# Expert probabilities in groups of four batches: one softmax in place over the probabilities' tile

## The chip, the core and the metric

The kernel runs on one core of a Trainium2 chip. The metric is device time in microseconds (us) of one execution. Engines: PE is TensorE, DVE is VectorE, ACT is ScalarE, POOL is GpSimd, SP is SyncE, whose queue issues most of the DMA.

## The reference, cut to what matters

x and ctx are 32 batches of 512 tokens by 512 features. Two residual steps follow each other:

```python
x = x + tanh(g_xattn) * xattn(layernorm(x), ctx, ctx)    # 8 heads, gated scores with a decay per position
x = x + tanh(g_ffn)   * experts(layernorm(x))

# in experts(), on xf = all 16384 rows:
logits = xf @ Wr + br                 # 8 experts
Sm = softmax(logits, axis=-1)
G_t, idx_t = top_k(Sm.T, n_tok // 8)  # each expert takes the 2048 rows with the highest probability
out = silu(xf[idx] @ W_up + b_up) @ W_down + b_down
y[idx] += G * out
```

The experts can choose only when the probabilities of all rows are known.

## The kernel before, in words

The program has two stages, each a block in which every engine runs its own hand-written instruction list; an engine enters the second block when all have left the first.

**Attention stage.** A batch is 4 tiles of 128 tokens. A loop of 34 iterations (`for i in range(NB + 2)`, NB = 32) works on several batches at once: in iteration i batch i is loaded and gets its first row moments, b1 = i-1 is turned and gets its gates, b2 = i-2 gets its scores and products, b3 and b4 are normalised, the finished rows of b5 = i-5 are turned (`turn_rows`) and multiplied by the router weights (`logits`), and b6 = i-6 gets its softmax. After the loop a written-out tail finishes the last batches. The order of work on every engine is that of the code. PE's outputs go through four shared PSUM banks; `iteration_fills` lists who fills which bank and which engine ("act" or "dve") empties it, and `fill` makes PE wait for that engine before the bank is filled again.

The softmax of a batch: PE computes the logits with experts along partitions (`logits`), ACT adds the bias (`logit_rows`, tile lg), PE turns them one iteration later (`turn_logits`, L689) into a bank with tokens along partitions. DVE takes the maximum of each row and subtracts it (`shifted_logits`, L921 and L922, tile lt, 128x32), ACT takes the exponential (`exponentials`, L436, tile ex), DVE sums, inverts and multiplies (`probabilities`, L927 to L929) into sm_all, which holds the probabilities of all 16384 rows as 128 x 128 x 8. SP stores each batch's part of it into the last 8 columns of the row scratch in DRAM (`store_probabilities`, L264): 512 pieces of 32 bytes.

Other names that the prediction uses: L281 and L285 load ctx (kraw) and x (xs) on SP, the first once PE has finished the last `chunk_state` (L777) of i-2; L903 is `row_moments` (bn_stats); L1006 and L1007 are `turned_gates`, which read what PE's `turn_gates` (L722 to L724) wrote; L915 is `head_sums`, L1035 `chunk_states` (tile S), L738 `scores`, L1052 and L1055 are in `gate_runs`. Scores of pair 1 wait for S, because they share the banks that S is read from.

**Expert stage.** PE turns the score columns of sm_all, DVE and PE select each expert's 2048 rows by rounds of counting, POOL gathers the rows with their probabilities (it waits for all row stores and all probability stores) and adds the results to the output; weights are loaded on SP and split by ACT, POOL and DVE into two parts each.

Of the kernel before, what the change touches and what calls it, by code (L numbers as in the profile page):

```python
# [26 lines left out]
AX = mybir.AxisListType  # L27
# [23 lines left out]
CRING = 3  # L51

# [36 lines left out]
def attention(nc, io, NB, dram, sm_all, tg, consts, stored, plan):  # L89
# [4 lines left out]
    xf_v = dram["xf"].rearrange("(b j p) w -> b p j w", j=TILES, p=P)  # L94
    ident, identb, ones = consts["ident"], consts["identb"], consts["ones"]
    with ExitStack() as ctx:
# [6 lines left out]
        def sem(name):  # L103
# [34 lines left out]
        lt = sb("lt", [P, TILES, NEXP]); mx = sb("mx", [P, TILES]); sx = sb("sx", [P, TILES]); ex = sb("ex", [P, TILES, NEXP])  # L138
# [11 lines left out]
                 "ldg rp x2t xf2v dchain achain pchain prep1 prep2 prep3").split()  # L150
# [9 lines left out]
        def iteration_fills(i):  # L160
            b1, b2, b5, b6 = i - 1, i - 2, i - 5, i - 6

            plan = [("qw", b2, 0, "dve", 0), ("q", b1, 0, "act", 1), ("k", b1, 0, "act", 2), ("q", b1, 1, "act", 3), ("k", b1, 1, "act", 1),
                    ("st", b2, 0, "act", 0), ("st", b2, 1, "dve", 2), ("st", b2, 2, "dve", 3), ("xfT", b5, 0, "act", 1),
                    ("qw", b2, 1, "dve", 0), ("scores", b2, 1, None, None), ("xfT", b5, 1, "act", 1),
                    ("xfT", b5, 2, "act", 0), ("q", b1, 2, "act", 2), ("k", b1, 2, "act", 3), ("q", b1, 3, "act", 1),
                    ("lt", b6, 0, "dve", 0), ("xfT", b5, 3, "act", 2), ("k", b1, 3, "act", 3),
                    ("qw", b2, 2, "dve", 1), ("scores", b2, 2, None, None), ("shift", b1, 0, "dve", 1), ("qw", b2, 3, "dve", 1),
                    ("gates", b1, 0, "dve", 0), ("lg", b5, 0, "act", 1), ("turn", b1, 0, "dve", 1)]
            if i >= NB + 2:  # L170
                free = [n for n in range(4) if n != {NB + 2: 0, NB + 3: 3, NB + 4: 2}[i]]
                plan = [("lt", b6, 0, "dve", 0)] if i == NB + 2 else []
                plan += [("xfT", b5, c, "act", free[c % 3]) for c in range(CH)]
                plan += [("lg", b5, 0, "act", free[1]), ("lt", b5, 0, "dve", {NB + 2: 3, NB + 3: 2, NB + 4: 3}[i])]
            return [f for f in plan if live(f[1])]
# [36 lines left out]
        def wait_taken(eng, kind, b, k):  # L212

            eng.wait_ge(*freed[kind, b, k])

# [32 lines left out]
        with nc.Block() as block:  # L248
            @block.sync
            def _(sp):  # L250
# [10 lines left out]
                def store_probabilities(b):  # L261
                    if 0 <= b < NB:
                        sp.wait_ge(s["smx"], b + 1)
                        sp.dma_start(xf_v[b][:, :, E_DIM:XW], sm_all[:, b * TILES:(b + 1) * TILES, :]).then_inc(s_probs, 16)  # L264
# [158 lines left out]
            def _(act):  # L423
# [9 lines left out]
                def exponentials(b):  # L433

                    wait_taken(act, "lt", b, 0)
                    act.activation(ex[:, :, :], lt[:, :, :], ACT.Exp).then_inc(s["lex"], 1)  # L436
# [113 lines left out]
                for i in range(NB + 2):  # L550
# [27 lines left out]
                    if live(b1):  # L578
                        turned("q", b1, 2)
                        turned("k", b1, 2)  # L580
                        turned("q", b1, 3)
                    if live(b5):
                        turned_rows(b5, 3)
# [5 lines left out]
                    if live(b6):  # L589
                        exponentials(b6)  # L590
# [39 lines left out]
                exponentials(a - 2)  # L630
# [3 lines left out]
                second_norm(a, (0, 1, 2, 3))  # L634
                for c in range(CH):
                    turned_rows(a, c)
                rsqrt_guess(NB + 3)
                second_norm(b, (0,))
                exponentials(a - 1)
                logit_rows(a)  # L640
                exponentials(a)
# [3 lines left out]
                exponentials(b)  # L645
# [235 lines left out]
            def _(dve):  # L881
# [42 lines left out]
                def probabilities(b):  # L924

                    dve.wait_ge(s["lex"], b + 1)
                    step(dve.tensor_reduce(sx[:, :], ex[:, :, :], AX.X, ALU.add))  # L927
                    step(dve.reciprocal(sx[:, :], sx[:, :]))
                    dve.tensor_tensor(sm_all[:, b * TILES:(b + 1) * TILES, :], ex[:, :, :], spread(sx[:, :], 2, NEXP), ALU.mult).then_inc(s["smx"], 1)  # L929
# [156 lines left out]
                for i in range(NB + 2):  # L1086
# [25 lines left out]
                    if live(b6):  # L1112
                        shifted_logits(b6)
# [22 lines left out]
                    if live(b6):  # L1136
                        probabilities(b6)
# [18 lines left out]
                shifted_logits(a - 2)  # L1156
# [330 lines left out]
def experts(nc, io, dram, sm_all, slots, weights, tg, consts, stored, plan, NTOK, K):  # L1487
# [7 lines left out]
    with ExitStack() as ctx:  # L1495
# [60 lines left out]
        with nc.Block() as block:  # L1556
# [21 lines left out]
            def _(pool):  # L1578
# [14 lines left out]
                pool.wait_ge(stored["probs"], 16 * (NTOK // SEQ))  # L1593
# [241 lines left out]
```

## Time and profile before

| what | value |
|---|---|
| median of three runs | 3066.34 us (3066.11 to 3068.3) |
| span of the profiled execution, first to last instruction | 3068.9 us |
| attention stage in it, until PE's first instruction of the expert stage | 1013.4 us |
| loop iterations 5 to 31, from one L915 to the next | 28.89 to 33.33 us |
| PE, DVE, ACT, POOL busy over the span | 96%, 60%, 37%, 34% |

Rows of the profile give the start of an instruction, its duration, engine, line, operation, output<-input and, in brackets, how long the engine was idle before it and what ended that. Durations of a group are means in ns. A matmul's end is modelled, so a busy PE can hide short stalls.

### The profile page before, as it was taken

What the parts mean: (1) busy time and instruction counts of PE and PEld (TensorE: products, weight loads), DVE (VectorE), ACT (ScalarE), POOL (GpSimd) and SP (SyncE); (2) the same over time, 40 slices, a digit from 0 to 9 for tenths busy, and PEclk for the clock granted to TensorE, in tenths of its full rate; (3) what the DMA queues carried; (4) which work ended last, traced back from release to release, by engine and by line L of the source; (5) the groups of instructions that cost most, each with busy time, mean ns of one, the idle gap of its engine ahead of it and who ended that gap; (6) DMA issues with size and microseconds to landing.
All of it is one profiled execution on the core that took longest, in us unless ns stands there. A gap on an engine that the chain in (4) does not pass through costs nothing.

```text
span 3068.9 us, 60770 instructions
## 1 busy us (share of the span) xinstructions
PE 2960.4 (96%) x24708; PEld 2392.9 (78%) x24708; DVE 1830.2 (60%) x5124; ACT 1136.7 (37%) x2025; POOL 1057.8 (34%) x1029
## 2 busy tenths in 40 slices
PE   6999999999998599999999999999999999999998
PEld 5888888888886377877777787777777777777886
DVE  6999899999888644354454444544445445443332
ACT  5778787777776321121121121122112112112110
POOL 4777677777767311121111111121112111121111
PEclk9999999999999699999999999999999999999999
DMA  3243443434342521241142231232123214222121
GB/s 130 84 167 128 152 144 136 167 112 167 113 166 85 147 51 34 36 100 32 40 105 35 49 79 34 37 87 70 31 37 84 49 30 110 37 49 58 35 37 24
DMA packets 140062, 250.70 MB, mean 82 GB/s; under 512 B 31456, under 2 KB 31456, under 8 KB 139784
## 3 DMA queue, kind: packets, MB, share of 16 engines
q1 hardware_dynamic: 105784, 170.80, 16.6%
q0 software_dynamic: 28672, 67.65, 12.6%
q10 hardware_dynamic: 5328, 8.36, 0.9%
q8 instruction: 197, 3.23, 0.4%
q14 instruction: 81, 0.66, 0.1%
HBM read 137.23 MB, written 101.19 MB: 78 GB/s over the span
## 4 chain that ended last, share of the span: by engine, by line
PE 64%; DVE 1%; DMA 1%; issue 0%; ACT 0%; POOL 0%; ACTq 0%; DVEq 0%; POOLq 0%
PE DN L1713 32%; PE UP L1687 31%; PE TT L1660 1%; DMA w_raw<-in_L_ffn_W_down 1%; DVE c_hit L1380 0%; PE c_bank L1373 0%; PE c_bank L1357 0%; DVE c_hit L1401 0%; DVE c_within L1396 0%; DVE down_lo L1246 0%; POOL out_x L1606 0%; ACT z L1631 0%; DVE c_gained L1433 0%; DVE c_begun L1395 0%; DVE mid_lo L1745 0%
## 5 line engine op out<-in xcount | busy, mean ns | idle before, releaser
L1606 POOL DMA_INDIRECT out_x<-y,slots x128 | 201.9, 1578 | 1631.2 <-DVE y L1767 1631.2
L1713 PE MATMUL DN<-down_hi,mid_hi 128*128 128x512 f32 x1408 | 577.9, 410 | 0.0
L1631 ACT ACTIVATE z<-UP,bup 128x512 f32<-128x512 f32 (+1 forms) x352 | 240.7, 686 | 857.6 <-PE UP L1687 838.5
L1687 PE MATMUL UP<-xT_hi,up_lo 128*128 128x512 f32 (+1 forms) x1408 | 555.5, 395 | 0.0
L1687 PE MATMUL UP<-xT_hi,up_hi 128*128 128x512 f32 (+1 forms) x1408 | 554.0, 394 | 1.2 <-DVE xT_lo L1724 0.9
L1687 PE MATMUL UP<-xT_lo,up_hi 128*128 128x512 f32 (+1 forms) x1408 | 552.1, 392 | 0.0
L1713 PE MATMUL DN<-down_lo,mid_hi 128*128 128x512 f32 x1280 | 505.5, 395 | 0.0
L1713 PE MATMUL DN<-down_hi,mid_lo 128*128 128x512 f32 x1280 | 505.4, 395 | 0.0
L1743 DVE CAST mid_hi<-z 128x512 fp32r<-128x512 f32 (+1 forms) x352 | 151.2, 429 | 486.0 <-ACT z L1631 485.8
L1615 ACT ACTIVATE xT_hi<-TT 128x512 fp32r<-128x512 f32 x126 | 75.0, 596 | 690.9 <-PE TT L1660 670.9
L1687 PEld LDWEIGHTS UP<-xT_hi,up_hi 128*128 128x128 f32 (+1 forms) x1408 | 260.2, 185 | 68.5 <-ACT z L1631 4.2
L1687 PEld LDWEIGHTS UP<-xT_lo,up_hi 128*128 128x128 f32 (+1 forms) x1408 | 259.8, 185 | 67.3 <-issue 0.3
L1687 PEld LDWEIGHTS UP<-xT_hi,up_lo 128*128 128x128 f32 (+1 forms) x1408 | 260.0, 185 | 65.5 <-issue 0.5
L1713 PEld LDWEIGHTS DN<-down_hi,mid_hi 128*128 128x128 f32 x1408 | 265.6, 189 | 51.3
L1713 PEld LDWEIGHTS DN<-down_hi,mid_lo 128*128 128x128 f32 x1280 | 240.4, 188 | 57.9
L1765 DVE TENSOR_TENSOR y<-DN,bdn 128x512 f32<-128x512 f32 x128 | 88.6, 692 | 329.0 <-PE DN L1713 325.6
L1713 PEld LDWEIGHTS DN<-down_lo,mid_hi 128*128 128x128 f32 x1280 | 241.1, 188 | 45.5
L1745 DVE TENSOR_TENSOR mid_lo<-z,mid_hi 128x512 fp32r<-128x512 f32 (+1 forms) x352 | 244.0, 693 | 12.1
L233 POOL TENSOR_TENSOR nsb<-nsb,rr 128x512 f32<-128x512 f32 x125 | 126.9, 1046 | 231.1 <-DVE nn L960 231.1
L1017 DVE SCALAR_TENSOR_TENSOR C<-QK,C 128x512 f32<-128x512 f32 x256 | 164.8, 685 | 8.6 <-PE QK L738 6.5
L903 DVE BATCH_NORM_STATS2 st<-xs 128x6 f32<-128x512 f32 x248 | 152.9, 679 | 20.6 <-DMA xs<-in_x 20.5
L738 PE MATMUL QK<-qT,kT 64*128 64x128 f32 x2048 | 148.8, 285 | 14.2 <-DVE S L1035 13.0
(264 smaller groups left out, 4983.7 us busy)
## 6 DMA issues: line engine op xcount, KB each, us to landing
xs<-in_x SPq DMA_DIRECT2D x32, 1024.0 KB, 8.4
kraw<-in_ctx SPq DMA_DIRECT2D x32, 1024.0 KB, 5.6
out_x<-xs SPq DMA_DIRECT2D x32, 1024.0 KB, 12.8
rows_scratch<-xfb SPq DMA_DIRECT2D x32, 1024.0 KB, 11.4
w_raw<-in_L_ffn_W_down SPq DMA_DIRECT2D x40, 512.0 KB
w_raw<-in_L_ffn_W_up SPq DMA_DIRECT2D x16, 682.5 KB
mid_hi<-mid_hi ACTq DMA_DIRECT2D x32, 86.0 KB
mid_lo<-mid_hi ACTq DMA_DIRECT2D x32, 84.0 KB
```

What stands on the lines that cost most here:

```text
L233: ins = eng.tensor_tensor(n, n, spread(scale[:, j, :], 2, DH), ALU.mult)
L738: mm = pe.matmul(QK[:, par, jj], kT[r, b % 2, p, jj], qT[r, b % 2, p, jj], start=True, stop=True)
L903: dve.bn_stats(st[:, which, j, :], src[:, j, :]).then_inc(s["dchain"], 1)
L1017: dve.scalar_tensor_tensor(out=c, in0=QK[:, par, :], scalar=DH ** -0.5, in1=c, op0=ALU.mult, op1=ALU.mult)\
L1606: pool.indirect_dma_start(out_rows, bass.IndirectOffsetOnAxis(ap=slots[:, m:m + 1], axis=0), y[:, t, :], None, compute_op=ALU.add).then_in ...
L1615: act.activation(xT[0][:, c, :], turned(n, c)[:, :], ACT.Copy).then_inc(s["thi"], 1)
L1631: act.activation(z[0:r, k % 2, :], UP[k % 3][0:r, :], ACT.Silu, bias=bup[0:r, e // 2, f:f + 1]).then_inc(s["z"], 1)
L1687: mm = pe.matmul(UP[k % 3][0:r, :], weights.up[wa][:, c, f * P:f * P + r], xT[xa][:, c, :], start=first, stop=(c == CH - 1 and wa == 1))
L1713: mm = pe.matmul(DN[m % 2][:, :], lhs, rhs, start=first, stop=(f == FCH - 1 and lhs is parts[-1][0]))
L1743: dve.tensor_copy(mid[0][0:r, f, :], z[0:r, k % 2, :]).then_inc(s["hi"], 1)
L1745: dve.tensor_tensor(mid[1][0:r, f, :], z[0:r, k % 2, :], mid[0][0:r, f, :].bitcast(FP32), ALU.subtract)\
L1765: dve.tensor_tensor(y[:, t, :], DN[m % 2][:, :], bdn[:, e % 2, :], ALU.add).then_inc(s["yp"], 1)
```

## The change

The softmax works on groups of four batches (SOFT = 4). For every batch ACT now copies the turned logits from the bank straight into the batch's part of sm_all (`raw_logits`); the bank is thus emptied by ACT, not by DVE. In every fourth iteration DVE and ACT do maximum, subtraction, exponential, sum, reciprocal and product over 128x128 elements in place in sm_all, and SP stores the four batches with one DMA of 2048 pieces of 32 bytes. In the tail the last group (batches 28 to 31) is done after the last batch's logits. The tiles lt and ex go away, and the wait of POOL's gather counts 8 stores instead of 32.

```diff
+    xf_t = dram["xf"].rearrange("(t p) w -> p t w", p=P)
...
-                    ("lt", b6, 0, "dve", 0), ("xfT", b5, 3, "act", 2), ("k", b1, 3, "act", 3),
+                    ("lt", b6, 0, "act", 0), ("xfT", b5, 3, "act", 2), ("k", b1, 3, "act", 3),
...
+        def logits_of(g):
+
+            return sm_all[:, g * SOFT * TILES:(g + 1) * SOFT * TILES, :]
...
                 def store_probabilities(b):
-                    if 0 <= b < NB:
-                        sp.wait_ge(s["smx"], b + 1)
-                        sp.dma_start(xf_v[b][:, :, E_DIM:XW], sm_all[:, b * TILES:(b + 1) * TILES, :]).then_inc(s_probs, 16)
+                    if b >= 0 and b % SOFT == SOFT - 1:
+                        g = b // SOFT
+                        sp.wait_ge(s["smx"], g + 1)
+                        sp.dma_start(xf_t[:, g * SOFT * TILES:(g + 1) * SOFT * TILES, E_DIM:XW], logits_of(g)).then_inc(s_probs, 16)
...
-                def exponentials(b):
-
-                    wait_taken(act, "lt", b, 0)
-                    act.activation(ex[:, :, :], lt[:, :, :], ACT.Exp).then_inc(s["lex"], 1)
+                def raw_logits(b):
+
+                    t = filled(act, "lt", b, 0)
+                    act.activation(sm_all[:, b * TILES:(b + 1) * TILES, :], t[:, 0:P].rearrange("p (j n) -> p j n", n=QD)[:, :, 0:NEXP], ACT.Copy)\
+                       .then_inc(s["ta"], 1)
+
+                def exponentials(g):
+
+                    act.wait_ge(s["lsh"], g + 1)
+                    act.activation(logits_of(g), logits_of(g), ACT.Exp).then_inc(s["lex"], 1)
...
                         turned("q", b1, 3)
+                    if live(b6):
+                        raw_logits(b6)
                     if live(b5):
                         turned_rows(b5, 3)
...
-                    if live(b6):
-                        exponentials(b6)
+                    if live(b6) and b6 % SOFT == SOFT - 1:
+                        exponentials(b6 // SOFT)
...
-                def shifted_logits(b):
-
-                    t = filled(dve, "lt", b, 0)
-                    l3 = t[:, 0:P].rearrange("p (j n) -> p j n", n=QD)[:, :, 0:NEXP]
-                    step(dve.tensor_reduce(mx[:, :], l3, AX.X, ALU.max))
-                    dve.tensor_tensor(lt[:, :, :], l3, spread(mx[:, :], 2, NEXP), ALU.subtract).then_inc(s["td"], 1)
+                def shifted_logits(g):
+
+                    wait_taken(dve, "lt", g * SOFT + SOFT - 1, 0)
+                    step(dve.tensor_reduce(mx[:, :], logits_of(g), AX.X, ALU.max))
+                    dve.tensor_tensor(logits_of(g), logits_of(g), spread(mx[:, :], 2, NEXP), ALU.subtract).then_inc(s["lsh"], 1)
...
+                def probabilities(g):
+
+                    dve.wait_ge(s["lex"], g + 1)
+                    step(dve.tensor_reduce(sx[:, :], logits_of(g), AX.X, ALU.add))
                     step(dve.reciprocal(sx[:, :], sx[:, :]))
-                    dve.tensor_tensor(sm_all[:, b * TILES:(b + 1) * TILES, :], ex[:, :, :], spread(sx[:, :], 2, NEXP), ALU.mult).then_inc(s["smx"], 1)
+                    dve.tensor_tensor(logits_of(g), logits_of(g), spread(sx[:, :], 2, NEXP), ALU.mult).then_inc(s["smx"], 1)
...
-                    if live(b6):
-                        shifted_logits(b6)
+                    if live(b6) and b6 % SOFT == SOFT - 1:
+                        shifted_logits(b6 // SOFT)
...
-                    if live(b6):
-                        probabilities(b6)
+                    if live(b6) and b6 % SOFT == SOFT - 1:
+                        probabilities(b6 // SOFT)
...
-                probabilities(a - 2)
-                shifted_logits(a - 1)
                 reciprocal_roots(NB + 3)
                 last_norm(b)
-                probabilities(a - 1)
-                shifted_logits(a)
-                probabilities(a)
-                shifted_logits(b)
-                probabilities(b)
+                shifted_logits(b // SOFT)
+                probabilities(b // SOFT)
...
-                pool.wait_ge(stored["probs"], 16 * (NTOK // SEQ))
+                pool.wait_ge(stored["probs"], 16 * (NTOK // (SEQ * SOFT)))
```

## Rows read from the trace of the kernel before

**Rows 1.** The page, busy time of each engine over the span.

```profile
PE 2960.4 (96%) x24708; PEld 2392.9 (78%) x24708; DVE 1830.2 (60%) x5124; ACT 1136.7 (37%) x2025; POOL 1057.8 (34%) x1029
```

**Rows 2.** Windows of single iterations: length, busy by engine, clock, DMA share, GB/s.

```profile
123.91:152.80 28.89, 28.89 (x488) 24.54 (x487) 26.46 (x73) 23.50 (x46) 22.09 (x23) 1.00 0.42 148
449.78:478.94 29.16, 28.79 (x490) 24.55 (x489) 27.27 (x79) 23.62 (x47) 21.68 (x23) 1.00 0.43 147
629.45:659.95 30.50, 29.40 (x491) 24.74 (x489) 27.55 (x78) 23.66 (x48) 21.15 (x23) 1.00 0.41 140
597.72:629.45 31.73, 30.38 (x487) 25.54 (x486) 27.58 (x79) 23.10 (x46) 22.39 (x23) 0.95 0.40 135
```

**Rows 3.** Waits from 152.8 to 968: total us, times, longest.

```profile
DVE st L903 <- DMA xs<-in_x: 15.6, 17, 1.9
PE QK L738 <- DVE S L1035: 11.5, 24, 0.6
```

**Rows 4.** Timeline of DVE in the iteration 449.78 to 478.94.

```profile
460.33 0.19 DVE L921 TENSOR_REDUCE mx<-T 128x4 f32<-128x32 f32 x1
460.75 2.47 DVE L903 BATCH_NORM_STATS2 st<-xs 128x6 f32<-128x512 f32 x4
...
474.94 0.18 DVE L927 TENSOR_REDUCE sx<-ex 128x4 f32<-128x32 f32 x1
475.37 0.19 DVE L929 TENSOR_TENSOR sm_all<-ex,sx 128x32 f32<-128x32 f32 x1
475.48 0.33 DVE L1006 COPY gb<-T 64x8 f32<-64x8 f32 x2
```

**Rows 5.** Timeline of PE in the same iteration.

```profile
453.86 1.16 PE L738 MATMUL QK<-qT,kT 64*128 64x128 f32 x16 [0.37 <-DVE S L1035]
...
459.24 0.27 PE L689 MATMUL T<-ident,lg 128*128 128x128 f32 x1
459.35 0.60 PE L672 MATMUL QK<-ident,xfb 128*128 128x128 f32 x4
...
462.80 0.43 PE L698 MATMUL T<-qT,gW 128*32 128x128 f32 x8
...
474.87 0.29 PE L724 MATMUL T<-steps,ones 128*128 128x16 f32 x2
```

**Rows 6.** DMA issues, single iterations (from 272.46, 451.4, 597): last number us to landing.

```profile
xs<-in_x SPq DMA_DIRECT2D x1, 1024.0 KB, 8.3
...
xs<-in_x SPq DMA_DIRECT2D x1, 1024.0 KB, 8.0
...
xs<-in_x SPq DMA_DIRECT2D x1, 1024.0 KB, 9.7
```

**Rows 7.** Groups by line, 152.8 to 968: total busy us, mean ns, idle before.

```profile
L935 DVE TENSOR_REDUCE ssq<-sq 128x8 f32<-128x512 f32 x110 | 74.7, 680 | 1.0
L929 DVE TENSOR_TENSOR sm_all<-ex,sx 128x32 f32<-128x32 f32 x27 | 9.1, 337 | 0.9
L522 ACT ACTIVATE low<-low 128x128 f32<-128x128 f32 x27 | 8.4, 310 | 0.9
L1052 DVE TENSOR_TENSOR rise<-T,cs 128x128 f32<-128x128 f32 x27 | 7.9, 292 | 5.0 <-PE T L706 4.1
```

**Rows 8.** Timeline of ACT, same iteration as rows 4.

```profile
460.53 0.65 ACT L441 ACTIVATE kT<-QK 128x512 f32<-128x512 f32 x1
```

**Rows 9.** Timeline of DVE at the end of the attention stage.

```profile
1011.28 0.19 DVE L921 TENSOR_REDUCE mx<-QK 128x4 f32<-128x32 f32 x1 [3.95 <-PE QK L689]
...
1012.43 0.19 DVE L929 TENSOR_TENSOR sm_all<-ex,sx 128x32 f32<-128x32 f32 x1
```

**Rows 10.** Timeline of SP's queue in the iteration of rows 4.

```profile
454.62 2.22 SPq L264 DMA_DIRECT2D rows_scratch<-sm_all  x1
```

**Rows 11.** DMA queues from 1010 to 1014: packets, MB, share of 16 engines.

```profile
q1 hardware_dynamic: 551, 0.02, 6.8%
```

**Rows 12.** Timeline of POOL: the first gather of the expert stage.

```profile
1040.91 1.27 POOL L1585 DMA_INDIRECT xg<-rows_scratch,slots  x1 [6.04 <-DVE slots L1408]
```

More of the change, by code:

```diff
@@ L51 @@
 CRING = 3
+SOFT = 4
 class Line:
@@ L137, in attention @@
         N1, N2 = TILES * HEADS, TILES * HEADS + TILES
-        lt = sb("lt", [P, TILES, NEXP]); mx = sb("mx", [P, TILES]); sx = sb("sx", [P, TILES]); ex = sb("ex", [P, TILES, NEXP])
+        mx = sb("mx", [P, SOFT * TILES]); sx = sb("sx", [P, SOFT * TILES])
         gwr = C[0:16, 0:3, :].rearrange("g n e -> g (n e)")
@@ L149, in attention @@
                  "ee dd qk cc af an sq sr x2 x2v lex smx hs vc uv "
-                 "ldg rp x2t xf2v dchain achain pchain prep1 prep2 prep3").split()
+                 "ldg rp lsh x2t xf2v dchain achain pchain prep1 prep2 prep3").split()
         s = {n: sem("a_" + n) for n in names}
@@ L171, in iteration_fills @@
                 free = [n for n in range(4) if n != {NB + 2: 0, NB + 3: 3, NB + 4: 2}[i]]
-                plan = [("lt", b6, 0, "dve", 0)] if i == NB + 2 else []
+                plan = [("lt", b6, 0, "act", 0)] if i == NB + 2 else []
                 plan += [("xfT", b5, c, "act", free[c % 3]) for c in range(CH)]
-                plan += [("lg", b5, 0, "act", free[1]), ("lt", b5, 0, "dve", {NB + 2: 3, NB + 3: 2, NB + 4: 3}[i])]
+                plan += [("lg", b5, 0, "act", free[1]), ("lt", b5, 0, "act", {NB + 2: 3, NB + 3: 2, NB + 4: 3}[i])]
             return [f for f in plan if live(f[1])]
@@ L629, in _ @@
                 rsqrt_guess(NB + 2)
-                exponentials(a - 2)
+                raw_logits(a - 2)
                 for c in range(CH):
@@ L634, in _ @@
                 second_norm(a, (0, 1, 2, 3))
+                raw_logits(a - 1)
                 for c in range(CH):
@@ L638, in _ @@
                 second_norm(b, (0,))
-                exponentials(a - 1)
                 logit_rows(a)
-                exponentials(a)
+                raw_logits(a)
                 for c in range(CH):
@@ L644, in _ @@
                 logit_rows(b)
-                exponentials(b)
+                raw_logits(b)
+                exponentials(b // SOFT)
             @block.tensor
@@ L915, in head_sums @@
                     dve.tensor_reduce(hs[:, :], kraw[:, b % VBUF, :, :].rearrange("p j (h d) -> p (j h) d", d=DH), AX.X, ALU.add).then_inc(s["hs"], 1)
-                def shifted_logits(b):
-                    t = filled(dve, "lt", b, 0)
-                    l3 = t[:, 0:P].rearrange("p (j n) -> p j n", n=QD)[:, :, 0:NEXP]
-                    step(dve.tensor_reduce(mx[:, :], l3, AX.X, ALU.max))
-                    dve.tensor_tensor(lt[:, :, :], l3, spread(mx[:, :], 2, NEXP), ALU.subtract).then_inc(s["td"], 1)
-                def probabilities(b):
-                    dve.wait_ge(s["lex"], b + 1)
-                    step(dve.tensor_reduce(sx[:, :], ex[:, :, :], AX.X, ALU.add))
+                def shifted_logits(g):
[5 more added lines that the diff above has]
+                    step(dve.tensor_reduce(sx[:, :], logits_of(g), AX.X, ALU.add))
                     step(dve.reciprocal(sx[:, :], sx[:, :]))
-                    dve.tensor_tensor(sm_all[:, b * TILES:(b + 1) * TILES, :], ex[:, :, :], spread(sx[:, :], 2, NEXP), ALU.mult).then_inc(s["smx"], 1)
+                    dve.tensor_tensor(logits_of(g), logits_of(g), spread(sx[:, :], 2, NEXP), ALU.mult).then_inc(s["smx"], 1)
                 def square_sums(b, p):
@@ L1155, in _ @@
                 row_variances(NB + 2)
-                shifted_logits(a - 2)
                 weigh_early(b, 3)
```

## The prediction, made before the changed kernel was run

> **What bounds the kernel now.** I read the busy shares first [rows 1]: PE works 96% of the span, so at most the rest can be won by work on other engines. The change touches only the attention stage (1013.4 of 3068.9 us); the expert stage after it runs the same instructions. So I cut the loop into iterations, from one L915 to the next, and read PE, DVE and DMA in each [rows 2].
>
> The reader should see two kinds of iteration. In the short kind (449.78) PE is busy 28.79 of 29.16 us and DVE 27.27. DVE looks nearly as full, but PE's only idle time is 0.37 us, at L738, where the scores wait for DVE's S [rows 2, 5]. In the long kind (629.45, 30.50 us) DVE stands 1.4 us waiting for the load of xs, and PE then idles for DVE's results. Over the whole loop the load costs DVE 15.6 us in 17 waits, and S costs PE 11.5 us in 24 [rows 3].
>
> The best evidence is iteration 5 (123.91), which has everything but the softmax, since no batch has come that far: 28.89 us, PE busy 28.89 [rows 2]. With the turning of the logits, 0.11 us on PE (459.24 to 459.35 in [rows 5]), an iteration without DVE's softmax would take 29.00 us. The short kind takes 29.16.
>
> The long kind follows the landing of xs. That load is issued about 0.9 us behind the ctx load, which waits for PE's L777, and landed 7.9 to 9.9 us after its issue in 25 loads: 9 by 8.2 us, 4 at 8.3, 3 at 8.6 to 8.7, 9 at 9.1 or later (8.0, 8.3 and 9.7 in [rows 6]). Iterations with 8.0 took 29.16, with 8.3 some 29.3, with 9.4 some 30.4. This cycle runs from L777 through both loads, DVE's row moments (L903), the variances, `gate_runs` and PE's work back to L777. DVE's `shifted_logits` lies ahead of its wait for xs, and `probabilities` lies where PE has work in hand up to L777. Neither is on that cycle.
>
> **What is removed from DVE.** `shifted_logits`: from 460.33 to 460.75, 0.42 us. `probabilities`: from 474.94 to 475.48, 0.54 us, up to about 0.8 where the product is longer, its mean being 0.337 against 0.19 here [rows 4, 7]. Together 0.96 us. There are 28 softmax iterations in the loop, 6 to 33; the seven with i = 9, 13 ... 33 get a group, 21 get nothing.
>
> What 0.96 us is worth is read at two places. After `probabilities` DVE does L1006, which needs PE's L724; that ended at 474.87 + 0.29 = 475.16. So DVE can come forward from 475.48 to about 475.20 and then stands: 0.28 us, not 0.54. From there to S nothing else waits, so PE's 0.37 at L738 falls by 0.28; by the floor of iteration 5 it is 29.16 - 29.00 = 0.16. I take 0.2, bounds 0.16 and 0.28. The 0.42 us ahead of row moments turns into a longer wait for xs, or into DVE waiting for PE's L706 (4.1 us already [rows 7]). Value: nothing; it is covered by PE, and if PE were faster it would be worth up to 0.42.
>
> So over the 21: nine PE-bound ones (i = 6, 7, 8, 14, 15, 16, 24, 26, 32) at 0.2 make 1.8 us; three with landings of 8.3 (10, 27, 30) at 0.1, since their cycle binds at about 29.2, make 0.3; nine bound by the load, nothing. Sum -2.1, bounds -1.4 and -3.4.
>
> **What is added on DVE.** Widening from 128x32 to 128x128. The reduction costs 191 ns for 32 elements and 680 for 512, which is 1.02 ns an element, so +0.10 for 96 more; the subtraction and the product go from 0.19 to the 0.292 of L1052 [rows 4, 7]. Reciprocal 4 to 16 elements: nothing visible. `probabilities` thus grows by 0.2 and `shifted_logits` by 0.2 in seven iterations. The first comes out ahead of S, where PE waits already: +0.2 in the PE-bound ones (9, 17, 25, 33), 0.8 us. In 13, 21, 29 it lies off the load's cycle. The second is covered by DVE's slack at L706 and L768. Bounds: 0 and, with 0.4 in all seven, 2.8.
>
> **What is added on ACT.** 28 copies of 128x32 at about the 0.25 us of the exponential they replace, now between q's third copy and the row copies, and in seven iterations an exponential of 128x128 at 0.310 (L522 in [rows 7]). PE next needs kT's last copy for the gates: it ended at 461.18, PE came at 462.80 [rows 5, 8]. Slack 1.6 us against 0.25: nothing. Behind it on ACT are the squares and the third C exponential, used by DVE only near 465; the bank becomes free earlier than before. DVE's group start waits for the fourth copy, which ACT does at about 460.06 to 460.31, as DVE arrives: 0 to 0.1, inside the bounds above.
>
> **SP and the stores.** The store behind a full queue holds SP for 2.22 us [rows 10]; four times the pieces hold it some 9. Behind it is only the next iteration's ctx load, 24 us later. Pieces are cheap: 551 packets took 6.8% of 16 engines for 4 us, 7.9 ns each [rows 11], so 2048 take 1.0 us. They come behind xs in the queue and leave its landing alone. Nothing, bounds 0 and 0.
>
> **The tail.** The earlier softmaxes there fell into DVE's wait for ACT and PE; no gain. The last one is serial. Before: from 1011.28 to 1012.62, 1.34 us [rows 9]. After: copy 0.25, maximum 0.28, subtraction 0.29, exponential 0.31, sum 0.28, reciprocal 0.18, product 0.29, and six hand-overs of 0.03 to 0.04, in all 2.1. So +0.75, bounds +0.5 and +1.1. The last store sends 2048 pieces ahead of the first weights. Even at 9 us for its descriptors the gather at 1040.91 is not held by it; the weights' split on POOL has 6.04 us of idle time before that gather [rows 12].
>
> **Sum.** -2.1 + 0.8 + 0.75 = -0.55 us, bounds -2.9 and +2.5 before the loads and PE's clock move. Those do: the same loads cost 0 or 1.5 us in neighbouring iterations for no reason that the rows show. The profiled span of 3068.9 is 2.6 above the median (its upper run 3068.3), so I apply the difference to the median: 3066.34 - 0.55 = 3065.8 us. Own range 3061 to 3070.5.
>
> **Rivals.**
>
> *DVE sets the loop.* Its 93% busy speaks for it. Then the whole is worth 21 x 0.96 = -20.2, groups 7 x 0.4 = +2.8, tail +0.75: -16.6, 3049.7 us. Against it: PE has 0.37 us left. Chance 0.08. The Trainium skill (VectorE: DVE Perf Modes, the TRN2 errata) says small instructions reading SBUF each pay a fixed extra time, to be mended by larger tiles; the trace agrees in size (191 ns for 32 elements, 680 for 512), and by that rule alone the time would be this rival's.
>
> *The loads fall better.* DVE and SP are freer in 21 iterations; if half of the 15.6 us of waits went, -7.8 - 0.55: 3058. For it: landings of 8.0 and 9.8 alternate. Against: nothing that the change moves stands ahead of xs. Chance 0.12.
>
> *Slower: the clock falls at the groups.* The 31.73 us iteration had PE idle 1.35 us and then PE at 1.2 instead of 2.4 GHz for part of it (mean 0.95); 629.45 had 1.1 idle and kept its clock [rows 2]. A group adds 0.2 to the wait at S. If that tips PE in all seven at 31.73 - 30.50 = 1.2 us each, +8.4, and -0.55: 3074. It decides where the idle time passes between 1.1 and 1.35 us. Against: four groups meet iterations with 0.4 idle. Chance 0.11.
>
> *Slower: the last store holds the weights.* If its descriptors hold SP 9 us (4 x 2.22), 3 beyond the 6.04 of slack [rows 10, 12]: +3 - 0.55, 3068.8. For an empty queue the issue is short. Chance 0.07. The Trainium skill (DMA: Bandwidth & Descriptors, Anatomy of one DMA) holds that many descriptors can be issued before their number costs; by it this is nothing.
>
> **Numbers.** The forecast has 0.62. A measurement of this kernel tells about 0.2% (6.1 us) from no change. Faster by more: 0.08 of the first rival, 0.08 of the loads, 0.01 of the forecast, 0.17. Slower by more: 0.09 of the clock, 0.02 elsewhere, 0.11. Same 0.72. Range 3056 to 3072 leaves out the first rival, part of the second, half of the clock's.
>
> **What would show it.** L921 to L929 seven times in the loop and once at the end, at 0.19 to 0.30; DVE waiting at L1006 for PE's L724; waits at L738 under 0.2 in non-group short iterations, of 29.0 us, and over 0.5 in groups; waits for xs above 15.6 in total; first PE instruction of the expert stage 0.5 to 1.1 later behind L689. Wrong if short iterations come out at 28.5 or less, if xs lands elsewhere, or if the clock falls in groups.

## The result, and the profile after

| kernel | median | range, runs | ratio to before (95%) | mean granted clock over its runs |
|---|---|---|---|---|
| before, beside it | 3068.41 us | 3063.15 to 3074.93, 20 | 1 | 0.9850 (85 runs beside the experiments) |
| after | 3073.62 us | 3064.09 to 3093.44, 20 | 1.002 (1.001 to 1.0029) | 0.9829 |

The change makes the kernel 0.2% slower, some 5 us; the forecast was 0.5 us faster and the time lies above the range. Of the 7.8 us between the forecast of 3065.8 and the measured time, 2.1 are the base: the forecast started from a median of three runs, 3066.34, and 20 runs of the same kernel give 3068.41. The other 5.7 are the change: some +5.2 where -0.55 was forecast.

The mean clock is that of TensorE over a whole run, 1 being 2.4 GHz. A straight line through the 20 runs of after gives -3.2 us for each +0.001 of it, and one through the 85 of before the same. On these lines, at a clock of 0.985, after takes 3068.2 us and before 3069.1: at an equal clock the change gains about 0.9 us, with a standard error of 1.1, which fits the sum and would also fit no gain at all. What is lost comes with the clock: 0.0021 lower, times 3.2, is 6.7 us. So the question is why this change lowers TensorE's clock.

The page of after, busy time: DVE has 120 instructions and 17 us less.

```profile
PE 2972.1 (97%) x24708; PEld 2400.6 (78%) x24708; DVE 1813.0 (59%) x5004; ACT 1137.2 (37%) x2033; POOL 1057.8 (34%) x1029
```

Windows of single iterations of after, columns as in [rows 2]. In this order: one that has no softmax yet, two without a group, one with a group, one without a group that is bound by the load, and two with a fall of the clock, the first of them with a group.

```profile
125.82:154.71 28.89, 28.89 (x488) 24.53 (x487) 26.46 (x73) 23.49 (x46) 22.01 (x23) 1.00 0.42 148
392.77:421.67 28.90, 28.48 (x487) 24.24 (x485) 26.53 (x73) 23.28 (x47) 21.43 (x23) 1.00 0.47 150
450.56:479.81 29.25, 29.04 (x489) 24.55 (x488) 26.52 (x73) 23.58 (x47) 22.20 (x24) 1.00 0.42 146
479.81:509.37 29.56, 29.46 (x492) 25.08 (x491) 27.65 (x78) 24.31 (x49) 21.95 (x23) 1.00 0.42 145
301.00:331.15 30.15, 29.12 (x489) 24.54 (x488) 26.45 (x73) 23.34 (x47) 21.68 (x23) 1.00 0.41 142
604.71:638.11 33.40, 32.16 (x489) 27.02 (x488) 27.94 (x79) 23.55 (x48) 21.80 (x23) 0.90 0.38 128
699.83:733.42 33.59, 32.18 (x489) 27.13 (x488) 26.53 (x73) 23.34 (x47) 22.83 (x24) 0.90 0.37 127
```

The reader should see that the short iterations did what was worked out: 28.90 us beside 29.16 in [rows 2]. Only six of the loop's 26 are under 29.0 us, though. The iteration at 699.83 has no group, and DVE is busy in it for 26.53 us, where it was 27.27 to 27.58 with a softmax in [rows 2]; yet PE needs 32.18 us for the work that took 29.12 at 301.00, since its clock is 0.90.

In the profiled execution of after the clock falls in six iterations of the loop, at 360.55, 540, 573, 605, 638 and 699.83; before it were three. Two of the six have a group, those at 360.55 and 604.71. The six keep PE busy for 188.8 us in all; at 29.12 each it would be 174.7. That makes 14.1 us; the three of before have 93.0 - 87.4 = 5.6 us.

Waits of after from 154.71 to 976: total us, times, longest.

```profile
DVE st L919 <- DMA xs<-in_x: 28.7, 21, 2.5
...
DVE gb L1021 <- PE T L740: 7.0, 22, 1.2
...
PE T L784 <- DVE rise L1067: 6.2, 8, 1.0
...
PE QK L754 <- DVE S L1050: 3.1, 5, 0.7
```

PE's wait for the scores has all but gone (11.5 us in 24 waits in [rows 3]). DVE now stands at `turned_gates` (L1021) for PE in 22 iterations, where it had one such wait, and for xs 28.7 us instead of 15.6. PE stands at `rise` for 6.2 us in 8 waits; before the change the same wait was this:

```profile
PE T L768 <- DVE rise L1052: 4.5, 7, 1.0
```

Timeline of DVE in the short iteration at 392.77: the wait at L1021 that the prediction names.

```profile
417.33 0.68 DVE L950 TENSOR_REDUCE ssq<-sq 128x8 f32<-128x512 f32 x1
418.20 0.34 DVE L1021 COPY gb<-T 64x8 f32<-64x8 f32 x2 [0.19 <-PE T L740]
```

Timeline of PE in the iteration at 699.83. Idle time before an instruction is in brackets.

```profile
719.24 0.45 PE L784 MATMUL T<-inner,selP 128*128 128x384 f32 x1 [0.97 <-DVE rise L1067]
719.90 0.60 PE L729 MATMUL T<-ends,later 128*128 128x8 f32 x2 [0.21 <-DVE ends L1070]
720.35 0.57 PE L730 MATMUL T<-unseen,ident 128*128 128x4 f32 x2
720.85 2.08 PE L754 MATMUL QK<-qT,kT 64*128 64x128 f32 x16
```

PE stands 0.97 us for DVE's `rise` and 0.21 for `ends`; right after that sixteen matmuls of L754 take 2.08 us. Sixteen of them at 416.61 in a short iteration take 1.05:

```profile
416.61 1.05 PE L754 MATMUL QK<-qT,kT 64*128 64x128 f32 x16
```

So PE went from 2.4 to 1.2 GHz within a microsecond of the wait. The falls of this loop come at this place, 18 to 22 us into an iteration; none comes in an iteration in which PE did not stand.

The whole profiled execution is 10.8 us longer (span 3079.7 against 3068.9). 1.9 us of it are there before the first softmax of the loop (this iteration begins at 154.71, not 152.80) and are chance; 6.9 come in its 26 iterations up to 939.80 (785.1 us against 778.2); 0.8 in the tail; the rest behind it. The falls' 14.1 us less the 5.6 of before are 8.5, more than the whole 6.9 of the loop.

Timeline of DVE at the end of the attention stage of after.

```profile
1020.25 0.28 DVE L936 TENSOR_REDUCE mx<-sm_all 128x16 f32<-128x128 f32 x1 [6.41 <-ACT sm_all L443]
1020.57 0.29 DVE L937 TENSOR_TENSOR sm_all<-sm_all,mx 128x128 f32<-128x128 f32 x1
1021.24 0.28 DVE L942 TENSOR_REDUCE sx<-sm_all 128x16 f32<-128x128 f32 x1 [0.37 <-ACT sm_all L449]
1021.56 0.25 DVE L943 RECIPROCAL sx<-sx 128x16 f32<-128x16 f32 x1
1021.85 0.29 DVE L944 TENSOR_TENSOR sm_all<-sm_all,sx 128x128 f32<-128x128 f32 x1
```

The same of ACT.

```profile
1020.02 0.20 ACT L443 ACTIVATE sm_all<-QK 128x32 f32<-128x32 f32 x1 [0.48 <-PE QK L705]
1020.90 0.31 ACT L449 ACTIVATE sm_all<-sm_all 128x128 f32<-128x128 f32 x1 [0.68 <-DVE sm_all L937]
```

From the copy's start to the product's end it is 1020.02 to 1022.14, 2.12 us, where 1.34 stood before.

### The profile page after: what moved, and what is told of

The parts are those of the page before. It is cut to its first block, busy times and chain, and to the rows that moved or that the text cites. A ratio compares the mean times of both kernels' runs of the same rounds, so it can differ in the third digit from the quotient of the medians.

```text
span 3079.7 us, 60633 instructions
## 1 busy us (share of the span) xinstructions
PE 2972.1 (97%) x24708; PEld 2400.6 (78%) x24708; DVE 1813.0 (59%) x5004; ACT 1137.2 (37%) x2033; POOL 1057.8 (34%) x1029
## 4 chain that ended last, share of the span: by engine, by line
PE 63%; DMA 2%; DVE 1%; issue 0%; ACT 0%; POOL 0%; ACTq 0%; DVEq 0%; POOLq 0%
PE DN L1722 32%; PE UP L1696 29%; DMA w_raw<-in_L_ffn_W_down 2%; PE TT L1669 1%; DVE c_hit L1389 0%; DVE down_lo L1255 0%; PE c_bank L1382 0%; ACT z L1640 0%; PE c_bank L1366 0%; DVE c_hit L1410 0%; DVE c_within L1405 0%; ACT down_hi L1249 0%; POOL out_x L1615 0%; DVE mid_lo L1754 0%; DVE c_gained L1442 0%
## 5 line engine op out<-in xcount | busy, mean ns | idle before, releaser
L1754 DVE TENSOR_TENSOR mid_lo<-z,mid_hi 128x512 fp32r<-128x512 f32 (+1 forms) x352 | 244.1, 693 | 12.1
L754 PE MATMUL QK<-qT,kT 64*128 64x128 f32 x2048 | 150.9, 288 | 7.5 <-DVE S L1050 4.4
```

What stands on the lines that cost most here:

```text
L754: mm = pe.matmul(QK[:, par, jj], kT[r, b % 2, p, jj], qT[r, b % 2, p, jj], start=True, stop=True)
L1754: dve.tensor_tensor(mid[1][0:r, f, :], z[0:r, k % 2, :], mid[0][0:r, f, :].bitcast(FP32), ALU.subtract)\
```

## The experiments

All times are medians. The experiments ran in three sets, each with "before" beside it: e1, e2, e3 and e5 (before 3068.2 us), e4, e6, e7 and e8 (3068.6), e9, e10 and e11 (3069.1); before's mean clock was 0.9849 to 0.9851 in all three, so clocks are compared across sets. The table puts the kernels in two sets; the sections after it tell the edits. "Wait at S" is PE's total before `scores` in the loop of the one profiled execution, "falls" are the iterations of its loop in which the clock fell.

| kernel | xs loaded | wait at S, us | falls | mean clock, runs | median us | ratio (95%) |
|---|---|---|---|---|---|---|
| before | late | 11.5 | 3 | 0.9850, 85 | 3068.6 | 1 |
| e5 | late | 12.1 | 2 | 0.9851, 12 | 3068.98 | 0.9997 (0.9983 to 1.0011) |
| e6 | late | 11.3 | 0 | 0.9847, 12 | 3071.49 | 1.0013 (1.0004 to 1.0022) |
| e9 | late | 10.8 | 0 | 0.9845, 12 | 3070.78 | 1.0006 (0.9994 to 1.0018) |
| e3 | late | 17.7 | 3 | 0.9847, 12 | 3077.53 | 1.0024 (1.0009 to 1.004) |
| after | late | 3.1 | 6 | 0.9829, 20 | 3073.62 | 1.002 (1.001 to 1.0029) |
| e4 | late | 4.2 | 2 | 0.9830, 11 | 3073.57 | 1.0015 (1 to 1.0029) |
| e8 | late | 2.8 | 5 | 0.9828, 12 | 3073.53 | 1.0016 (1.0003 to 1.0029) |
| e2 | first | 10.9 | 0 | 0.9859, 12 | 3059.45 | 0.9965 (0.9952 to 0.9978) |
| e1 | first | 4.8 | 1 | 0.9850, 12 | 3059.29 | 0.9969 (0.9955 to 0.9984) |
| e10 | first | 2.4 | 1 | 0.9848, 9 | 3058.99 | 0.997 (0.9957 to 0.9982) |
| e11 | first | none | 2 | 0.9847, 7 | 3058.76 | 0.9969 (0.9952 to 0.9985) |
| e7 | first | none | 1 | 0.9853, 6 | 3055.26 | 0.9962 (0.9948 to 0.9977) |

A mean clock has a standard error of 0.0003 to 0.0006 (0.00016 for before). The three kernels with xs late and little wait at S stand at 0.983; the five that have this wait at 0.985. The falls are those of one execution each, and e4, e6 and e9 happened to be profiled in a good one: its clock was 0.987 in all three, far above the means of 0.9830, 0.9847 and 0.9845. So their 2, 0 and 0 falls are not typical, and the argument rests on the mean clocks.

### e1 and e2: after and before with x loaded first

```diff
 for i in range(NB + 2):
+    if XBUF <= i < NB: ... sp.dma_start(xs[:, i % XBUF, :, :], x_v[i]) ...
     if VBUF <= i < NB: ... sp.dma_start(kraw[:, i % VBUF, :, :], c_v[i]) ...
-    if XBUF <= i < NB: ... sp.dma_start(xs[:, i % XBUF, :, :], x_v[i]) ...
```

> The changed kernel, but SP issues the load of x ahead of the load of ctx. Lump theory: in the changed kernel PE no longer waits for S (L738 before, L754 now), so in iterations held up by the load of xs it reaches the wait for DVE's rise sooner, the idle time comes in one piece of about 1.0 us, and the clock falls to 1.2 GHz more often (7 iterations of 31.4 to 33.6 us against 3). With x first, xs lands some 6.5 us after the loads begin instead of 9 to 10.6, there are no long iterations and no falls in the loop: iterations of 28.9, three in four, and about 29.4 in a group, some 3046 us, clock above 0.987, and a few us faster than the kernel before with the same edit. Group theory (the wide operations or the large stores themselves cost the 5 us): the changed kernel stays some 5 us slower than the kernel before with the same edit.

> The kernel before, with the load of x issued ahead of that of ctx. Both theories: the waits for xs (15.6 us) vanish, and iterations take 29.16: about 3048 to 3050 us. Lump theory: the changed kernel with this edit is 2 to 5 us faster than this one. Group theory: about 5 us slower than this one.

Measured: 3059.29 and 3059.45 us. Both theories had the times 9 to 13 us too low: the waits for xs are gone, and most iterations are short, but a few pieces in which PE's own sequencer held it and falls of the clock remain. Windows of e1, a short iteration and one with a fall:

```profile
276.77:305.67 28.90, 27.81 (x478) 23.73 (x474) 26.54 (x74) 22.60 (x45) 21.41 (x23) 1.00 0.45 150
213.06:246.17 33.11, 32.06 (x489) 27.25 (x488) 26.72 (x74) 23.69 (x47) 22.06 (x23) 0.90 0.38 129
```

And one of e2, a short iteration:

```profile
331.26:360.40 29.14, 28.78 (x489) 24.54 (x488) 27.18 (x78) 23.60 (x47) 21.78 (x23) 1.00 0.44 147
```

What follows is in their difference, and it is neither theory's: with xs late the change costs 5 us, with xs in time -0.2, where the one theory had 2 to 5 us faster and the other 5 slower. So the loss of time isn't in the softmax by itself (a group's width, the copies, the tail); it needs the late load beside it. In the x-first pair the clock too is lower with the change, by 0.0009 with an error of 0.0004 (+2.9 us), and the shorter iterations pay for that. So the late load makes the loss of clock larger; it isn't the whole of it. (The expectation counts seven long iterations in after; the trace has six with a fall.)

### e5: the new code with groups of one batch

The copies on ACT, the softmax in place and the store of after, but for every batch, at before's places.

```diff
-SOFT = 4
+SOFT = 1
```
(and the tail's calls of `exponentials`, `shifted_logits` and `probabilities` for each of the last batches, as before has them.)

> The changed kernel with groups of one batch: ACT copies the turned logits into the probabilities' tile and every softmax is done in place for each batch at the places of the kernel before, in the tail too, with a store for each batch. Lump and group theories both: as the kernel before, 3067 to 3070. If ACT's copy ahead of the row copies is what costs, it stays near 3073.

Measured: 3068.98 us, clock 0.9851, and the wait at S 12.1 us in 25. ACT as the bank's reader and the work in place cost nothing. This is the change without its batching, and time and clock are before's; what costs lies in the batching.

### e8: the removal alone

e5, in which the loop makes the sum, reciprocal and product for one batch of four only; the other three batches' probabilities are stored as undivided exponentials. Maximum, subtraction and exponential stay for every batch.

```diff
+def NORM(g):
+    return g % 4 == 3 or g >= 28
...
-                    if live(b6) and b6 % SOFT == SOFT - 1:
+                    if live(b6) and NORM(b6):
                         probabilities(b6 // SOFT)
```

> The kernel with groups of one, whose time was that of the kernel before, without probabilities (sum, reciprocal, product) for three of four batches in the loop: their exponentials are stored without being divided by their sum. No wide operation, no large store, no longer tail. Lump theory: short iterations of the three 28.9, PE's wait at S gone there, longer waits at rise where xs is late, mean clock 0.983 to 0.984, and 3068 to 3072 although 0.5 us of DVE's work went 21 times. Group theory: 3063 to 3065.

Measured: 3073.53 us and 0.9828. Work was taken away from e5 and nothing added, neither wide operations nor a long tail, and it is 4.5 us slower. That is above both theories' times. The means of the two differ by 4.2 us with an error of 2.0, their clocks by 0.0023 with an error of 0.0006: the clock is the firmer sign. A row of the waits of e8:

```profile
PE QK L764 <- DVE S L1060: 2.8, 6, 0.6
```

Windows of e8, one short iteration and one with a fall:

```profile
391.61:420.50 28.89, 28.60 (x488) 24.36 (x486) 26.83 (x75) 23.52 (x48) 20.89 (x22) 1.00 0.44 148
420.50:452.87 32.37, 30.71 (x489) 25.71 (x488) 26.94 (x76) 23.48 (x48) 22.70 (x24) 0.95 0.40 133
```

### e3, e6 and e4: work put back into after

In the 21 iterations without a group, DVE gets work on scratch tiles: e3 a sum, a reciprocal and a product of 128x32 where `probabilities` was; e6 one reduction of 384 elements at that place; e4 a maximum and a subtraction of 128x32 where `shifted_logits` was. The edits, shortened:

```diff
                     if live(b6) and b6 % SOFT == SOFT - 1:
                         probabilities(b6 // SOFT)
+                    elif live(b6):
+                        idle_probabilities(n)      # e3; idle_reduction in e6
...
                     if live(b6) and b6 % SOFT == SOFT - 1:
                         shifted_logits(b6 // SOFT)
+                    elif live(b6):
+                        idle_shift(n)              # e4
```

> The changed kernel, and in the 21 iterations without a group DVE does the reduction, the reciprocal and the product of 128x32 on scratch tiles where the softmax of a batch had them, ahead of turned_gates. Nothing reads them. Lump theory: PE waits for S again (some 0.4 us in short iterations), the wait for rise in long ones is 0.2 to 0.3 us shorter, the clock falls about as often as before, short iterations take 29.16, and the time is that of the kernel before plus the longer groups and tail, at 3069 to 3070: below the changed kernel although DVE does more. Group theory: no gain, 3074 to 3078.

Measured: 3077.53 us with the clock back at 0.9847. The time was missed because the product didn't take 0.19 us. Timeline of e3, one row of POOL and then DVE around it:

```profile
448.89 1.19 POOL L253 TENSOR_TENSOR xs<-xs,nsb 128x512 f32<-128x512 f32 x1
...
448.95 0.18 DVE L953 RECIPROCAL dm<-dm 128x4 f32<-128x4 f32 x1
449.16 0.97 DVE L954 TENSOR_TENSOR dy<-dx,dm 128x32 f32<-128x32 f32 x1
450.06 0.33 DVE L1041 COPY gb<-T 64x8 f32<-64x8 f32 x2
```

It started while POOL worked on xs (448.89 + 1.19 = 450.08) and ended with it (449.16 + 0.97 = 450.13). Eight of the 21 products took 0.95 to 1.20 us. That made many iterations 29.9 us long. So e3 gives the clock's answer and not the time's, and e6 put in an operation with one input.

> The changed kernel with one reduction of 384 elements (about 0.55 us, one input, no product) on DVE ahead of turned_gates in the 21 iterations without a group; nothing reads its result. It has no product that POOL can hold up, which made the fill of the earlier run cost 0.97 us in place of 0.19. Lump theory: short iterations 29.16 with 0.4 us of waiting at S, the waits at rise shorter, mean clock back from 0.983 to 0.985, time 3068 to 3070, below the changed kernel by 4 us with more work on DVE. Group theory: clock stays at 0.983 and the time at 3074 or above.

Measured: 3071.49 us, clock 0.9847, no fall in the loop. With 11.5 us more work on DVE the median is 2.1 us under after's. That alone is no proof, as the two intervals overlap; the clock's step of 0.0018, with an error of 0.0006, is. The median is 1.5 us above what was expected: the short iterations are 29.20 us, longer than before's 29.16. Waits of e6 in the loop:

```profile
PE QK L755 <- DVE S L1057: 11.3, 25, 0.7
...
PE T L785 <- DVE rise L1074: 3.3, 5, 0.9
```

Windows of e6, a short iteration and one bound by the load:

```profile
393.40:422.61 29.21, 28.50 (x487) 24.45 (x487) 27.01 (x74) 23.31 (x47) 22.11 (x23) 1.00 0.46 149
362.48:393.40 30.92, 29.53 (x493) 24.82 (x491) 27.88 (x78) 23.97 (x49) 22.18 (x24) 1.00 0.39 138
```

The second window, with a group, is the telling one. Timeline of PE in it:

```profile
366.56 1.16 PE L755 MATMUL QK<-qT,kT 64*128 64x128 f32 x16 [0.32 <-DVE S L1057]
...
381.63 0.45 PE L785 MATMUL T<-inner,selP 128*128 128x384 f32 x1 [0.86 <-DVE rise L1074]
382.29 0.39 PE L730 MATMUL T<-ends,later 128*128 128x8 f32 x2 [0.21 <-DVE ends L1077]
```

PE stands 1.07 us at `rise` and `ends`, more than in after at 540 (0.96), where the clock fell. It has stood 0.32 at S fifteen microseconds ahead of it, and its clock stays at 1.00.

> The changed kernel with the maximum and the subtraction of 128x32 on scratch tiles in the 21 iterations without a group, at the place where shifted_logits of a batch was, ahead of the row moments; nothing reads them. Lump theory: nothing, since this time lies in DVE's wait for xs and in its wait for PE at rise; clock 0.983, 3073 to 3076, non-group short iterations 28.9. If the loss were that DVE runs ahead at this place, the clock would be 0.985 and the time 3068.

Measured: 3073.57 us, clock 0.9830. DVE's work ahead of the row moments costs and guards nothing that can be told from the noise, as the prediction said of it; it is the place ahead of S that counts. (e4's clock lies 0.0017 under e6's, with an error of 0.0007.)

### e9: e8 with the reduction of e6

> The kernel of e8 (no probabilities for three of four batches in the loop) with one plain reduction of 384 elements (about 0.55 us of VectorE) put ahead of turned_gates in the 21 iterations that lost them. Leaves out what e8 leaves out: three of four batches' probabilities stay undivided exponentials. Theory (the wait of PE at S guards the clock): the wait at S comes back at about 0.4 us, the mean clock goes from 0.983 to 0.985, and the time is about 3069, 4 us under e8 although VectorE does 11.5 us more. Rival (work is only work; the clock goes by chance): the time stays at 3073 or rises to 3076, the clock at 0.983.

Measured: 3070.78 us, 0.9845, no fall in the loop and 10.8 us of wait at S. The clock comes back a second time, with a different kernel under it: 0.0017 above e8's, with an error of 0.0007. The time by itself is no proof (2.7 us under e8, with errors of 1.4 and 1.6), nor did it reach the 3069 that was expected; its short iterations are 29.20, as in e6.

### e10: e8 with x loaded first

> The kernel of e8 with x's load issued ahead of the context's. Leaves out what e8 leaves out. Theory (the lost wait at S costs clock only where xs comes late): with xs in time there is nothing for PE to stand at behind it, the iterations without probabilities take 28.9 us, the clock is 0.985 to 0.986 and the time 3054 to 3056, under e2's 3059.5. Rival (fewer waits at S cost clock wherever x is): the clock is 0.983 and the time 3060 to 3064.

Measured: 3058.99 us and 0.9848. Taking the work out costs 4.5 us with xs late (e8 against e5) and nothing beside e2 with xs in time (e5 with x first, its exact partner, wasn't run; e2 is the nearest). It isn't the 3054 to 3056 that was expected; nor is it the rival's 3060 to 3064. Its clock is 0.0011 under e2's, with an error of 0.0003, half of what the removal costs with xs late: the rival, that fewer waits at S cost clock wherever x is, is right in part, and the shorter iterations make up for it in time.

### e7 and e11: nothing of the softmax between rise and S

Both load x first and make `probabilities` one iteration later, at the place of `shifted_logits`: e7 with groups of four, e11 with groups of one. Nothing is left out.

```diff
-                    if live(b6) and b6 % SOFT == SOFT - 1:
-                        probabilities(b6 // SOFT)
...
                     if live(b6) and b6 % SOFT == SOFT - 1:
                         shifted_logits(b6 // SOFT)
+                    if b6 >= SOFT and b6 % SOFT == 0:
+                        probabilities(b6 // SOFT - 1)
```
(e11 calls `probabilities(b6 - 1)` ahead of `shifted_logits(b6)`.)

> The changed kernel with the load of x first, and the sum, reciprocal and product of a group moved one iteration on, to where shifted_logits stands, since with x first DVE waits about 1.0 us in all for ACT and PE behind that place. Lump theory: every iteration 28.9, seven times 0.55 us less than with x first alone, 3055 to 3056, clock 0.985 to 0.986. Group theory: as with x first alone, 3059.

> The kernel of e5 (groups of one batch) with x's load issued ahead of the context's, and each batch's sum, reciprocal and product made one iteration later, in shifted_logits' place ahead of the row moments' end; nothing is left out. Theory: with xs in time and nothing of the softmax between rise and S, every iteration takes about 28.9 us, the clock is 0.985, the time 3054 to 3056, as e7. Rival (VectorE's operations at the early place move the wait of PE to rise): iterations of 29.2 and more, 3059 to 3062, as e2.

Measured: 3055.26 us (6 runs) and 3058.76 us (7 runs). e7 came as expected, e11 3 to 5 us above the 3054 to 3056 that was expected of it, its short iterations at 29.02 and not 28.9; the intervals of the two overlap. In e7 nearly every iteration takes 28.9 us. What is left are rare holds of PE that wait for no engine. Windows of e7, a plain iteration and one with a hold:

```profile
595.42:624.31 28.89, 28.78 (x489) 24.54 (x488) 26.93 (x76) 23.78 (x48) 21.20 (x22) 1.00 0.43 148
503.00:537.18 34.18, 32.25 (x489) 27.16 (x488) 27.36 (x76) 23.69 (x47) 22.74 (x24) 0.90 0.39 127
```

PE's timeline in the last:

```profile
521.70 0.43 PE L815 MATMUL A<-S,qw 64*128 64x65 f32 x2 [1.83 <-issue]
```

e7 is the version that beats both kernels: 0.9962 of before (0.9948 to 0.9977), some 12 us. Some 9 of them are the order of two loads (e1 and e2). What the move of `probabilities` adds isn't settled: 4 us in e7, under 1 in e11.

## Why the prediction was wrong, point by point

**The step that failed.** "nine bound by the load, nothing" (their share of the sum), and with it the condition of the rival "the clock falls at the groups". The prediction read rightly that time won ahead of S can't shorten an iteration whose cycle runs through the load, and took that for no effect. But the time stays in the iteration. PE no longer stands 0.3 to 0.6 us at S (11.5 us in 24 waits became 3.1 in 5); it stands longer at `rise`, 15 us later (4.5 us in 7 waits became 6.2 in 8), and the clock falls there, six times where it was three. The rival put the fall into the seven group iterations, through work *added* ahead of S, and made it hang on the iteration's whole idle time, 1.1 to 1.35 us. It has come from work *removed*, in four of six cases in iterations without a group (699.83 is one), and the fall at 540 came at 0.96 us of idle time in all:

```profile
559.31 0.65 PE L784 MATMUL T<-inner,selP 128*128 128x384 f32 x1 [0.96 <-DVE rise L1067]
```

The rival was right that a stand of PE of about 1 us can tip the clock; its place was wrong, its price of 1.2 us a fall too low (1.6 us of PE's time at 573.28, 3.0 at 540), and its chance of 0.11 with them. That its 3074 us is the measured time to within half a microsecond is luck: it had seven falls more at 1.2 us each, and a base that was 2.1 us too low; the trace has three more, at 8.5 us together.

**How firm this is.** That the removal ahead of S is what costs the clock is shown from both sides, with xs late: taking it away alone (e8 against e5) brings 0.9851 to 0.9828; putting work back there brings 0.983 to 0.9845 or 0.9847 three times (e3, e6, e9); putting it back ahead of the row moments doesn't (e4). That it costs nothing in time once xs is early is shown by e1 against e2 and by e10, to within an error of 1.4 us; it costs some clock even there.

Why a wait at S guards the clock is less firm. In the profiled executions of all thirteen kernels there are 50 iterations in which PE stood 0.65 us or more, in pieces over 0.12 us, 17 to 22 us into the iteration. Where it had also stood 0.25 us or more at its beginning, the clock fell in 5 of 21; where it hadn't, in 20 of 29. Part of this is length, since the second lot stood longer: of the stands of 0.95 us and more the clock fell in 4 of 7 and in 17 of 20, of the shorter ones in 1 of 14 and in 3 of 9. And a plainer reading isn't excluded, that PE just stands less at `rise` where it stands at S: in the loop it stood there 4.5, 3.3, 1.5, 1.3 and 0.4 us in before, e6, e9, e3 and e5, and 6.2, 4.9 and 2.2 us in after, e8 and e4. The idle time's length alone doesn't sort the falls, though: 1.07 and 1.09 us in e6 kept the clock, 0.65 in after at 573.28 did not. Nor is the count of falls in one profile proof: e4 shows two with the same mean clock as after. What in PE's record decides stays open.

**The terms of the sum.** The short iterations were right in direction and low in size: 28.90 instead of 29.16, -0.26, where I took 0.2 of the bounds 0.16 and 0.28. The floor of 29.00 was too high by the turning of the logits, which doesn't show in the length. A group in the short kind costs +0.4 over 29.16 (29.56 at 479.81), not 0.2, and 0.66 over the new short kind. Timeline of DVE in this iteration:

```profile
505.10 0.28 DVE L942 TENSOR_REDUCE sx<-sm_all 128x16 f32<-128x128 f32 x1
505.41 0.25 DVE L943 RECIPROCAL sx<-sx 128x16 f32<-128x16 f32 x1
505.70 0.29 DVE L944 TENSOR_TENSOR sm_all<-sm_all,sx 128x128 f32<-128x128 f32 x1
```

The reduction and the product are as long as was worked out. The reciprocal is 0.07 longer than the narrow one, where I had "nothing visible". From the sum's start to the copy behind the product it is 0.81 us instead of 0.54, and PE's next wait at S is 0.64 instead of 0.37: that is 0.27 of the 0.4, and the rest stays open. In three of the six groups of the loop the product was longer, up to 0.76 us with a mean of 0.426 over the six, since it met POOL (L944 below). The tail was +0.8 (predicted +0.75). At an equal clock all of it comes to -0.9 us with an error of 1.1, against -0.55.

Groups by line of after, 154 to 970:

```profile
L443 ACT ACTIVATE sm_all<-T 128x32 f32<-128x32 f32 x27 | 6.3, 232 | 0.0
L944 DVE TENSOR_TENSOR sm_all<-sm_all,sx 128x128 f32<-128x128 f32 x6 | 2.6, 426 | 0.2
```

The price of the narrow operations went by size as said. The Trainium skill (VectorE: DVE Perf Modes, the TRN2 errata section) would merge them. The trace agrees that 32 narrow sums at 0.18 us cost more than eight at 0.28. What is saved had no buyer, since PE, at 97% busy, gives the time.

**What was hidden stayed hidden.** The copies take ACT 0.23 us (L443 above) and PE never came to wait for them. `shifted_logits` was worth nothing where it stood (e4). The wait at L1021 for PE came as said, in 22 iterations. Waits for xs grew above 15.6, as said, to 28.7. The stores are harmless, and that rival is out. The store's line on SP's queue in after:

```profile
L271 SPq DMA_DIRECT2D rows_scratch<-sm_all x8: 360/1752/2267, 276.8 to 1022.2; - x8
```

POOL's first gather of after:

```profile
1050.41 1.27 POOL L1594 DMA_INDIRECT xg<-rows_scratch,slots  x1 [6.62 <-DVE slots L1417]
```

Eight stores of 2048 pieces hold SP 0.36 to 2.27 us each (the three numbers are the least, the median and the longest, in ns), no longer than one of 512 pieces did [rows 10]; my 9 us for four times the pieces was wrong. The gather stands 6.62 us for DVE's slots, so no store holds it. The Trainium skill (DMA: Bandwidth & Descriptors, Anatomy of one DMA) says of DMAs that GpSimd issues that many descriptors can be emitted before their number costs. These stores are issued by SP, so that sentence of the Trainium skill doesn't quite cover them; the trace shows the same for them, with 0.36 us for the last store.

**The other rivals.** DVE doesn't set the loop: 17.2 us of its work went, and the short iterations got 0.26 us shorter, not 0.96. The loads fell no better (8.5 us from issue to landing in the median of all 32, 8.4 before); the waits for them grew.

## What to carry to other kernels

Before costing a removal at nothing because its iteration is bound elsewhere, ask where the engine with a clock to lose will stand instead: here 0.4 us less at one place and more at a later one came with a loss of 0.2%, although DVE had 120 instructions fewer to do. Compare mean clocks over many runs, not only times: a step of 0.002 was clear at 12 runs where the times overlapped, and it pointed to the cause. And move the late load first: swapping two issue lines was worth 9 us (0.3%), which no arithmetic on the softmax could give.

## What the runs showed of the hardware that was not expected

**A product on DVE can last until POOL's operation ends.** Alone, the product of 128x32 with both inputs in SBUF takes 0.19 us. Started while POOL works on SBUF tiles it ended with POOL's operation: in e3 at 450.13 against 450.08 (0.97 us), and in the kernel before at 625.60 + 0.47 = 626.07 against 624.83 + 1.18 = 626.01. The reductions and the reciprocal beside it kept 0.18 us. So it was with 16 of the 27 products in before's loop: each ended within 0.06 us of a POOL operation on 128x512 that was under way when it started, and took 0.21 to 0.55 us; the other 11 took 0.19. Rows of the kernel before:

```profile
624.83 1.18 POOL L246 TENSOR_TENSOR xs<-xs,nsb 128x512 f32<-128x512 f32 x1
...
625.17 0.18 DVE L927 TENSOR_REDUCE sx<-ex 128x4 f32<-128x32 f32 x1
...
625.60 0.47 DVE L929 TENSOR_TENSOR sm_all<-ex,sx 128x32 f32<-128x32 f32 x1
```

The Trainium skill (SBUF — State Buffer, SBUF: two separate sides) says that the pair of ports that the two engines share is locked for a whole instruction and that a VectorE operation with two SBUF inputs needs it; the trace agrees. I had read the mean of 0.337 us in [rows 7] as a longer product without asking what made it longer.

**TensorE's clock falls around quite short waits.** PE went from 2.4 to 1.2 GHz after standing 0.65 to 1.8 us, and once, in e5, after 0.45. A fall cost its iteration about 1.6 us of extra PE time at a mean clock of 0.95 and 3 us at 0.90. With a short wait some 15 us ahead of it, a stand of 0.65 us or more passed without a fall in 16 of 21 cases. I had not thought that a wait at one place could spare the clock at another; that it does is suggested by these counts and not shown, since these stands were shorter too.
